# A mixture-of-experts gate whose product keeps the tokens still instead of the gate weights

## The reference, cut to what matters

```python
logits = tokens.astype(jnp.float32) @ gate_weight.astype(jnp.float32).T   # [2048, 8]
probs = jax.nn.softmax(logits, axis=-1)
top1 = jnp.argmax(logits, axis=-1)
mask = jax.nn.one_hot(top1, E, dtype=jnp.int32)
ranks = jnp.cumsum(mask, axis=0) - 1
mask = mask * (ranks < C)                       # C = 320 places per expert
```

## Time and profile before

| | |
|---|---|
| median of 3 runs | 1296.1 us (1295.58 to 1296.44) |
| profiled execution: span from the first to the last instruction | 1299.9 us |
| its own time outside the span | not in the page |
| TensorE, matmuls / loads | 1085.2 us busy (83%) / 997.7 us (77%) |
| VectorE | 737.3 us (57%) |
| ScalarE | 564.6 us (43%) |
| GpSimd | 101.1 us (8%) |
| mean granted TensorE clock | 0.918 |
| routing of the first layer, up to the last scatter's landing | about 12 to 65 us of the span |
| routing of the second layer | about 757 to 795 us |

### The profile page before, as it was taken

The page is one execution under the profiler, slowest core; times in us unless marked ns, Lnnn a source line. Parts: engine busy times, 40 slices in busy tenths (PEclk is TensorE's granted clock), DMA queues, the critical chain, the costliest instruction groups (busy, mean ns, idle before and its releaser), DMA issues.

```text
span 1299.9 us, 20268 instructions
## 1 busy us (share of the span) xinstructions
PE 1085.2 (83%) x7618; PEld 997.7 (77%) x7619; DVE 737.3 (57%) x1205; ACT 564.6 (43%) x879; POOL 101.1 (8%) x140
## 2 busy tenths in 40 slices
PE   5369495879899999859999991798999999789495
PEld 2169495879899999847778740797999999789495
DVE  5536163546566677538687752354677677545252
ACT  4335242435445566434343241344565565434141
POOL 2500000000000000010000023000000000000000
PEclk9779698898999999969999995798999999989798
DMA  9757453354464665140000026253665665625130
GB/s 263 225 199 269 164 189 115 121 181 151 151 214 163 215 222 183 32 141 1 1 33 33 33 106 240 68 178 124 215 224 173 212 221 182 203 88 178 41 118 20
DMA packets 91094, 191.35 MB, mean 147 GB/s; under 512 B 4656, under 2 KB 5168, under 8 KB 90928
## 3 DMA queue, kind: packets, MB, share of 16 engines
q1 hardware_dynamic: 84976, 170.82, 40.1%
q0 software_dynamic: 6016, 18.97, 4.2%
HBM read 161.34 MB, written 32.62 MB: 149 GB/s over the span
## 4 chain that ended last, share of the span: by engine, by line
PE 78%; issue 10%; DMA 3%; POOL 3%; DVE 1%; SPq 1%; ACT 1%; POOLq 0%; DVEq 0%; ACTq 0%
PE acc L1038 13%; PE acc L1040 13%; PE acc L1039 13%; PE psH L1038 12%; PE psH L1039 11%; PE psH L1040 11%; PE psT L1130 3%; POOL disp L454 2%; DMA disp<-zeros 2%; PE psT L1171 1%; SPq L315 1%; DMA dtok<-disp 1%; PE psT L1246 1%; PE psH L1171 1%; ACT xT L648 0%
## 5 line engine op out<-in xcount | busy, mean ns | idle before, releaser
L1038 PE MATMUL psH<-dth,wih 128*128 128x240 f32 (+5 forms) x1024 | 303.8, 297 | 113.2 <-issue 113.2
L1039 PE MATMUL psH<-dtl,wih 128*128 128x240 f32 (+5 forms) x1024 | 302.0, 295 | 0.0
L1040 PE MATMUL psH<-dth,wil 128*128 128x240 f32 (+5 forms) x1024 | 301.4, 294 | 0.0
L1038 PE MATMUL acc<-hth,woh 128*128 128x240 f32 (+5 forms) x1024 | 296.4, 289 | 0.0
L1039 PE MATMUL acc<-htl,woh 128*128 128x240 f32 (+5 forms) x1024 | 293.3, 286 | 0.0
L1040 PE MATMUL acc<-hth,wol 128*128 128x240 f32 (+5 forms) x1024 | 293.2, 286 | 0.0
L1038 PEld LDWEIGHTS psH<-dth,wih 128*128 128x128 f32 x1024 | 201.7, 197 | 113.5 <-issue 113.5
L593 ACT ACTIVATE gel<-psH 128x320 f32<-128x320 f32 x256 | 110.9, 433 | 300.3 <-PE psH L1040 299.9
L722 DVE TENSOR_TENSOR wol<-raw_wo,woh 128x1024 fp32r<-128x1024 f32 x128 | 156.7, 1224 | 106.8 <-ACT woh L572 106.8
L876 DVE CAST hth<-gel 128x640 fp32r<-128x640 f32 x128 | 63.2, 493 | 259.6 <-ACT gel L593 259.6
L1039 PEld LDWEIGHTS psH<-dtl,wih 128*128 128x128 f32 x1024 | 202.0, 197 | 2.6 <-issue 2.6
(11 more groups left out here) (158 smaller groups left out, 1176.7 us busy)
## 6 DMA issues: line engine op xcount, KB each, us to landing
raw_wi<-in_wi SPq DMA_DIRECT2D x64, 1024.0 KB, 5.6
raw_wo<-in_wo SPq DMA_DIRECT2D x64, 1024.0 KB, 5.2
dtok<-disp SPq DMA_DIRECT2D x18, 516.0 KB, 3.9
disp<-zeros SPq DMA_DIRECT2D x4, 1287.5 KB, 21.6
out_x<-xt SPq DMA_DIRECT2D x4, 1024.0 KB, 4.3
xt<-in_x SPq DMA_DIRECT2D x3, 1024.0 KB, 14.2
xt<-x SPq DMA_DIRECT2D x3, 1024.0 KB, 12.0
dtok<-disp SPq DMA_DIRECT2D x18, 129.0 KB, 4.3
```

The source lines that it names most:

```text
L1038: pe.matmul(out, lh, rh, start=first, stop=False)
L1039: pe.matmul(out, lh, rl, start=False, stop=False)
L1040: return pe.matmul(out, ll, rh, start=False, stop=last)
```

## The change

The gate product is written the other way round. For each of the 4 tiles of a group and each of the 4 chunks, the 128 x 128 block of transposed tokens is the stationary operand, and the 128 x 8 gate weights stream past it. The logits come out with 128 tokens on partitions and 8 experts per tile, in the place where `logits_by_tokens` put them. So `lgT`, `ps_logitT`, VectorE's copy to `lgT`, the four transposes, `logits_by_tokens` and the two semaphores `lgT_copied` and `lg_turned` go. A group's product has 16 calls of `matmul` instead of 4.

```diff
-        ps_logitT = [acc[k][0:E, :] for k in (0, 1)]
         ps_logit = [acc[k][:, 0:GROUP * E] for k in (0, 1)]
...
                 if new:
                     dve.wait_ge(s.logits_done, g + 1)
-                    dve.tensor_copy(lgT[:, :], ps_logitT[a]).then_inc(s.lgT_copied, 1)
-                    dve.wait_ge(s.lg_turned, g + 1)
                     dve.tensor_copy(lg[:, :, :], ps_logit[a].rearrange("p (t e) -> p e t", e=E)
                                     ).then_inc(s.lg_copied, 1)
...
                     if g >= 2:
                         pe.wait_ge(s.lg_copied, g - 1)
-                    for c in range(DC):
-                        ins = pe.matmul(ps_logitT[g % 2], small[:, GATE0 + c * E:GATE0 + (c + 1) * E],
-                                        xTt[:, g % 2, c, :], start=(c == 0), stop=(c == DC - 1))
+                    for j in range(GROUP):
+                        for c in range(DC):
+                            ins = pe.matmul(ps_logit[g % 2][:, j * E:(j + 1) * E],
+                                            xTt[:, g % 2, c, j * P:(j + 1) * P],
+                                            small[:, GATE0 + c * E:GATE0 + (c + 1) * E],
+                                            start=(c == 0), stop=(c == DC - 1))
                     ins.then_inc(s.logits_done, 1)
-
-                def logits_by_tokens(g, s=s):
-                    pe.wait_ge(s.lgT_copied, g + 1)
-                    for j in range(GROUP):
-                        ins = pe.transpose(ps_logit[g % 2][:, j * E:(j + 1) * E], lgT[:, j * P:(j + 1) * P],
-                                           ident[0:E, 0:E])
-                    ins.then_inc(s.lg_turned, 1)
...
                         logits(g)
                         if g + 1 < GROUPS:
                             turn(g + 1)
-                        logits_by_tokens(g)
                     if g >= 1:
                         ranks(g - 1)
...
                 logits(0, nxt)
-                logits_by_tokens(0, nxt)
```

More of the change, by code:

```diff
@@ L160, in build_kernel @@
         xTt = at("xTt", [P, 2, DC, GT], F32, a_xTt)
-        lgT = put("lgT", [E, GT], F32)
         each = [P, E, GROUP]
@@ L195, in __init__ @@
                 self.logits_done = sem(f"logits_done{n}")
-                self.lgT_copied = sem(f"lgT_copied{n}")
-                self.lg_turned = sem(f"lg_turned{n}")
                 self.lg_copied = sem(f"lg_copied{n}")
```

## The result

| | before | after |
|---|---|---|
| median of the runs, us | 1296.27 (1295.58 to 1297.84, 4 runs) | 1308.78 (1306.5 to 1311.63, 4 runs) |
| span of the profiled execution, us | 1299.9 | 1309.8 |
| first gate product to token transposes, first layer | 17.01 to 69.4 | 17.31 to 75.84 |
| first expert of the first layer starts | 79.60 | 87.66 |
| last attention product of the second layer ends, gate product starts | 756.76 | 769.08 |

The ratio after to before is 1.010, 95% interval 1.0081 to 1.012. The forecast was 1289.7 us, range 1286.5 to 1296: wrong in sign, outside the range, and beyond the slowest of its rivals (1301.4) too.

A forecast was written before the change was run, and what follows sets the result against it. It took the second routing stage as bound by TensorE, ScalarE and VectorE up to `to_row` of the second group, then by GpSimd's scatters. Sum: -4.4 - 2.7 + 0.7 = -6.4 from 1296.1, so 1289.7 us, range 1286.5 to 1296.

The forecast's parts named there:

- Part 2: Gate product of one group after the change: 32 load-and-matmul pairs at 0.075 us each, 2.4 us where it took 3.60.
- L: Time of one group's new gate product on TensorE, taken as 2.4 us; gain in the second layer gone at 4.05.
- rival B: Gate product: 0.107 to 0.137 us a pair, gain 1.9 to loss 1.0 in the stage, 1292.2 to 1295; chance 0.09.
- rival A: Gate product: slow loads lie open at 0.19 us each, TensorE bounds the second routing, 1301.4 us, slower; chance 0.07.
- rival C: Second layer's routing: TensorE's clock falls to 1.2 GHz from 760 us on, 1292.4 to 1295.6, middle 1294; chance 0.08.
- Part 1: First layer's routing: no change, scatters have cover of 1.5 us on the first group and 7 on the last.
- Part 3: Second layer's routing chain to the scatters: turn(3) and what follows come 4.4 us earlier, one GpSimd wait of 1.2 left.
- Part 4: Place of TensorE's code: 2.7 us before expert 1 of the second layer gone, 0.7 charged for new stalls at jumps.
- rival D: Experts' code falls badly: two more jumps find their target missing, 4.5 us each, 1298.7 us; chance 0.06.

The follow-up runs named there:

- wide128: The changed kernel with 128 columns streamed past each whole load instead of 8: 1296.24 us against 1300.19 for the kernel before, ratio 0.9975.
- new_first: The kernel before with the new gate product in the first layer alone, plus 48 dummy products there: 1304.24 us against 1300.19, ratio 1.0031.
- wide64: The changed kernel with 64 columns streamed past each whole load instead of 8: 1304.6 us in one profiled run.
- swap: The kernel before with group 0's turn back in the second layer issued behind group 1's gate product: 1298.94 us against 1300.19, ratio 0.998.
- pad_second: The kernel before with 80 dummy products (160 instructions) in the second layer alone: 1295.55 us against 1298.33, ratio 0.9977.
- pad_both: The kernel before with 80 dummy products (160 instructions) in each of both layers: 1300.1 us against 1297.37, ratio 1.0024.
- new_second: The kernel before with the new gate product in the second layer alone, plus 48 dummy products there: 1305.67 us against 1300.19, ratio 1.0039.
- after_realigned: The changed kernel with 48 dummy products added in each layer: 1307.45 us against 1297.37 for the kernel before, ratio 1.0087.
- split32: The changed kernel with each load cut into four of 32 tokens: 1307.9 us in one profiled run.
- split64_timed: The changed kernel with each load cut into two of 64 tokens, 8 columns streamed: 1305.88 us against 1298.34 for the kernel before, ratio 1.0054.
- split64_wide64: The changed kernel with two loads of 64 tokens and 64 columns streamed past each: 1295.41 us, ratio 0.9971 to the kernel before.

## Why the prediction was wrong, step by step

Two steps failed: Part 2's price of a pair, and the clock of 2.4 GHz that Parts 1 to 3 take for granted. The second made the loss.

- **Part 2, the price: "I take 0.075 us a pair, L = 32 x 0.075 = 2.4 us."** Measured: 0.112 us at 2.4 GHz and 0.213 at 1.2 (L = 3.6 and 6.8). Two choices led there. The nearest row was the turn back of `lgT`, a 128-column float32 load with 8 columns; but that is a transpose, and its load fills 8 rows of the array and not 128. Its four loads in the kernel before take 0.32 us with the last one's 0.137 in it, (0.32 - 0.137) / 3 = 0.061 us from one to the next (weight loads of the kernel before, in order of time):

```profile
26.33 0.32 PEld L1088 LDWEIGHTS acc<-ident,lgT 8*128 8x128 f32 x4 [0.29 <-issue]
```

  Whether the transpose or the 8 rows make it cheap, no run separates. And the load's record (88 ns for 8 columns, 137 in the turn) was read as its price; it is a length from start to end, and records overlap. The interval rival B named (0.107 to 0.137) holds the value at 2.4 GHz.
- **The row that was there.** Part 2 says that the trace has no such pair, and rival A that no row has this load in the open. The experts' products in the kernel before have it. Matmuls of expert 3, and the clock there in the columns of the earlier trace rows:

```profile
294.03 0.41 PE L1038 MATMUL psH<-dth,wih 128*128 128x240 f32 x1
294.24 0.41 PE L1039 MATMUL psH<-dtl,wih 128*128 128x240 f32 x1
294.45 0.41 PE L1040 MATMUL psH<-dth,wil 128*128 128x240 f32 x1
```

```profile
293.60:295.30 1.70, 1.70 (x9) 1.70 (x9) 0.00 (x0) 0.00 (x0) 0.00 (x0) 0.50 0.00 0
```

  They come 0.213 us apart, each with a load of 128 columns (the kernel declares these operands float32r, the view prints f32). Where 288 and 320 columns stream at the same clock the steps are 0.240 and 0.267 us, one cycle a column; by that 240 columns would take 0.200. The 0.213 is the load's, to the nanosecond the pair of the kernel after. At 2.4 GHz the same products come 0.112 us apart.
- **The Trainium skill was nearer.** Its page TensorE: Matmul & The Clock Gate, LDWEIGHTS, gives columns divided by 1.2 GHz, 107 ns. At 2.4 GHz the trace has 0.112 us, and with 64 and 96 columns 0.058 and 0.085 where 53 and 80 ns follow from it. At 1.2 GHz, where the same pair takes 0.213 us, it does not hold.
- **What lost the forecast: the clock, rival C in kind.** Parts 1 to 3 are reckoned at 2.4 GHz throughout. With the true pair at that clock (L = 3.65 by the group of `wide128`) Part 3 still gains 1.3 us, and the sum is 1296.1 - 1.3 - 2.0 = 1292.8, within the range; `wide128`, which has that pair and mostly keeps the clock, is level with the kernel before or little faster. The granted clock fell in the second stage, at 773.1, and in the first did not rise until 39.2 us, so groups of 7.00 and turns of 3.75. I gave rival C 0.08 and 1294, because I gave it my pair of 0.075 and looked for it in the second layer alone.
- **Part 1, "nothing": its condition failed, not its reading.** The cover was 1.5 us on the first group, and "about 1 us longer per group" the limit; the groups got 3.4 us longer, and the scatters waited for `to_row`. That is 8.1 us at the first expert's start (7.2 in the profile of `new_first`, of which 4.5 are left at the attention's end) and 4.0 in the total of `new_first`.
- **Part 3, the chain, was right.** With L = 7.31 / 2 = 3.65, the group of `wide128` with its clock held, it says that turn(3) starts at 759.9 + 10.95 = 770.85, 1.3 us earlier than 772.11. Measured in `wide128`: 768.67, 13.94 us behind the first gate product, where the chain says 14.09. The stages of `wide64` and `wide128` came out 1.3 and 1.7 us shorter. The 1.16 us of the removed wait are worth about 0.9 in the stage by `swap`.
- **Part 4, code.** The 2.7 us gone before expert 1 of the second layer: right (6.38 to 3.35, and `pad_second` makes it faster by 2.8 us with nothing else). The charge of 0.7 for new stalls was too small: rival D's mechanism cost 4.4 us in the first layer, at one jump. Together the two are +1.4 us by these profiles and 3.1 (0.1 to 6.0) by the timing of `pad_both`, where the sum had -2.0.

In the profiles the sum runs: +8.1 at the first expert, +4.3 in experts 3 to 7 of the first layer (+12.3 at the attention's end), +3.4 in the second stage, -5.1 from its first expert's start to the third's (822.1 to 941.2 before, 837.8 to 951.8 after; 3.0 of it the shorter gap), -0.7 in the rest: +9.9. The medians are 12.5 apart. This profile's second stage is a mild one: 46.9 us, where `new_second` and `after_realigned`, with the same product, have 50.2 and 52.4.

## What to carry to other kernels

Before swapping the operands of a float32 product so that few columns stream past many loads, price the pair by the step between ordinary products with that very load, at either clock (here the experts' products had it), not by a transpose and not by the length of a load's record; if there is none, make the test. Ask of every such change what it does to the clock in the coldest place that it touches, for a slower pair there is multiplied by two, and the work around it too. If the tokens must be stationary, loads of 64 columns into two halves of the output, with as many columns streamed past them, beat both kernels here (0.9971 of before, 0.9953 to 0.9988).

## What the runs showed of the hardware

- Ordinary float32 loads into the same output partitions follow each other in 64, 128, 192 and 256 cycles at 1.2 GHz with 32, 64, 96 and 128 columns loaded, and in 0.032, 0.058, 0.085 and 0.112 us at 2.4. With 128 loaded the step is the same for 8, 64 and 128 columns streamed.
- Pairs for the two halves of the output partitions run side by side: 64 pairs of 64 columns take 4.19 us at 1.2 GHz, where one behind another they would take 6.8.
- The granted clock with the same loads: 0.50 from 763.1 on with 8 columns streamed, 1.00 up to 783.1 with 64 (second routing, loads of 64). In the first layer all eight profiles with 8 columns there show most of 16 to 50 us at 1.2 GHz; those of the old product, and the three with as many columns streamed as loaded, show most of it at 2.4.
- The view of stretches prints 1.00 where the clock has no record yet. The pace of like instructions (7.00 us a group at 17 and at 48 us) tells which clock it was.
- Moving code by 160 instructions moved 3 to 8 us between jumps; the same program had 0.5 and 8.3 us before two experts in one execution, 3.9 and 0.5 in another. Short pairs in large numbers (128 instructions in 2.7 us) came with waits under "issue" of up to 1.2 us between two of them in the last group of the first layer (`split32`, `split64_timed`, `split64_wide64`); that instructions are late there is a likely reading and not shown.
